# Key-query products on two 64-row halves of TensorE, with masked queries made once by ScalarE and VectorE, in an attention and expert kernel

## What is computed

```python
q = layernorm(x); k = v = ctx
ig, fg = gate projections of [q, k, v]           # per head and token
cs = cumsum(log_sigmoid(fg))
log_D = where(s >= t, cs[s] - cs[t], -inf) + ig[t]
m = max(log_D, axis=t)
qk = einsum('hsd,htd->hst', qh, kh) / sqrt(DH)   # DH = 16
C = qk * exp(log_D - m)
n = maximum(abs(sum(C, t)), exp(-m))
h = einsum('hst,htd->hsd', C / (n + EPS), vh)
x = x + layernorm(h) * ln_scale
x = x + experts(layernorm(x))                    # top 2 of 8, three layers, exact gelu
```

## Time and profile before

| | us |
|---|---|
| Median of 3 runs | 223.58 |
| Lowest and highest run | 218.94, 224.69 |
| Span of the profiled execution | 219.7 |

### The profile page before, as it was taken

The page is one execution under the profiler, slowest core; times in us unless marked ns, Lnnn a source line. Parts: engine busy times, 40 slices in busy tenths (PEclk is TensorE's granted clock), DMA queues, the critical chain, the costliest instruction groups (busy, mean ns, idle before and its releaser), DMA issues.

```text
span 219.7 us, 2995 instructions
## 1 busy us (share of the span) xinstructions
PE 180.9 (82%) x973; PEld 135.5 (62%) x973; DVE 156.7 (71%) x428; ACT 84.9 (39%) x160; POOL 128.5 (58%) x133
## 2 busy tenths in 40 slices
PE   7768899979999953676999999898998989999100
PEld 3464355554665722225999999696987969888000
DVE  2836243864866889927989999999999999955100
ACT  2352473430233011007366665727466374422100
POOL 6795033442501569474728787886978876445370
PEclk9969999975788555589999999999999999999855
DMA  5494019999920110010101120311203120021230
GB/s 163 118 364 143 12 28 339 375 371 360 358 69 1 49 38 10 0 49 16 30 0 31 15 28 22 30 30 13 32 19 30 30 25 8 5 30 12 24 26 5
DMA packets 19530, 18.16 MB, mean 83 GB/s; under 512 B 2232, under 2 KB 14008, under 8 KB 19512
## 3 DMA queue, kind: packets, MB, share of 16 engines
q1 hardware_dynamic: 15440, 15.22, 21.0%
q0 software_dynamic: 3712, 2.62, 9.1%
q10 hardware_dynamic: 360, 0.09, 0.2%
HBM read 15.07 MB, written 2.75 MB: 81 GB/s over the span
## 4 chain that ended last, share of the span: by engine, by line
DVE 42%; PE 29%; issue 15%; POOL 5%; DMA 4%; ACT 2%; SPq 0%; DVEq 0%; ACTq 0%; POOLq 0%
DVE wlo L917 12%; PE bank L1029 7%; PE bank L1060 7%; PE bank L1165 6%; DVE g1l L904 5%; DVE g2l L904 5%; DVE g1h L907 4%; POOL out_rows L438 3%; DVE g2h L907 3%; DVE qn L664 2%; DMA out_rows<-ys,ids 2%; PE bank L1004 2%; DMA xs<-in_x 2%; PE bank L1048 2%; PE bank L1049 2%
## 5 line engine op out<-in xcount | busy, mean ns | idle before, releaser
L438 POOL DMA_INDIRECT out_rows<-ys,ids x24 | 39.5, 1645 | 23.3 <-DVE ys L929 14.7
L578 ACT ACTIVATE g<-bank,smt 128x320 f32<-128x320 f32 x64 | 31.0, 527 | 52.4 <-PE bank L1165 35.0
L1165 PE MATMUL bank<-g1h,whi 128*128 128x320 f32 x128 | 41.7, 326 | 4.1 <-DVE g1l L904 3.9
L1165 PE MATMUL bank<-g1l,whi 128*128 128x320 f32 x128 | 39.5, 309 | 0.0
L1165 PE MATMUL bank<-g1h,wlo 128*128 128x320 f32 x128 | 39.5, 308 | 0.0
L917 DVE TENSOR_TENSOR wlo<-wraw,whi 128x512 fp32r<-128x512 f32 x32 | 32.7, 1064 | 0.8 <-ACT whi L535 0.8
L425 POOL DMA_INDIRECT xg<-xn_rows,ids x24 | 26.2, 1091 | 9.1 <-issue 5.5
L1165 PEld LDWEIGHTS bank<-g1h,whi 128*128 128x128 f32 x128 | 24.0, 188 | 8.5 <-issue 8.5
L383 POOL TENSOR_TENSOR wlo<-wraw,whi 128x512 fp32r<-128x512 f32 x16 | 24.2, 1525 | 7.7 <-ACT whi L535 7.6
L535 ACT ACTIVATE whi<-wraw 128x512 fp32r<-128x512 f32 x48 | 27.6, 623 | 0.3 <-issue 0.3
L904 DVE TENSOR_TENSOR g2l<-g,g2h 128x320 fp32r<-128x320 f32 x32 | 23.3, 729 | 1.1
(11 more groups left out here) (160 smaller groups left out, 306.1 us busy)
## 6 DMA issues: line engine op xcount, KB each, us to landing
wraw<-in_L_ffn_W SPq DMA_DIRECT2D x8, 1024.0 KB, 9.0
wraw<-in_L_ffn_W SPq DMA_DIRECT2D x16, 256.0 KB, 8.8
xs<-in_x SPq DMA_DIRECT2D x2, 256.0 KB, 3.6
cs_in<-in_ctx SPq DMA_DIRECT2D x2, 256.0 KB, 4.5
out_rows<-x SPq DMA_DIRECT2D x8, 64.0 KB, 2.1
xn_rows<-qn SPq DMA_DIRECT2D x8, 64.0 KB, 1.9
xg<-xn_rows,ids POOLq DMA_INDIRECT x24
out_rows<-ys,ids POOLq DMA_INDIRECT x24
```

What stands on the lines that cost most here:

```text
L438: g.indirect_dma_start(out=out, out_offset=bass.IndirectOffsetOnAxis(ap=ids[0:n, col:col + 1], axis=0), in_=ys[0:n, e % 2, c, :], in_offse ...
L578: a.activation(dst[:, m, :], bank[m][:, 0:MAIN], ACT.Gelu, bias=smt[:, col + MC * e + m:col + MC * e + m + 1]).then_inc(done, 1)
L1165: last = t.matmul(dst, wcol(w, p, layer, k, m), act_(k), start=(n == 0), stop=(n == 3 * ks - 1))
```

## The change

The masked queries of all batches are made once, ahead of the loop, as `qm`, with four head slots instead of eight: in slot h the rows of head h (in the upper 64 rows) and of head h + 4 (in the lower 64) stay, so each half of the rows carries four heads. The mask `hpick` has a column per slot. ScalarE makes batches 0 to 3 from PSUM bank 3, VectorE batches 4 to 7 from bank 4. `logits` runs two products of 64 rows, one on each half of the rows, each still 512 columns. `LT` and `RH` are 128 rows high, the rows from 27 on zero; GpSimd clears both whole, then writes ones in LT's first 27 rows. `select_heads` is moved on ScalarE. `hn` and `hl` use qT's space and `x2` that of `cs_in`. Several semaphores are merged into one with other counts (three scans into `scan_done`, four steps into `den_done`); these hunks are left out below.

```diff
-        LT = at("LT", [3 * NH + 3, B, S], BF16)
-        RH = at("RH", [3 * NH + 3, BH, S], BF16)
+        LT = at("LT", [128, B, S], BF16)
+        RH = at("RH", [128, BH, S], BF16)
         delta = at("delta", [3 * NH, NH])
-        qbd = at("qbd", [128, 2, NH, S])
+        qm = at("qm", [128, NH // 2, B, S])
...
-        hn = at("hn", [128, 2, 2, D])
-        hl = at("hl", [128, 2, 2, D])
+        hn = qT[:, 0:4, :].rearrange("p (a i) d -> p a i d", i=2)
+        hl = qT[:, 4:8, :].rearrange("p (a i) d -> p a i d", i=2)
...
-        x2 = at("x2", [128, B, D])
+        x2 = cs_in
...
                             pattern=[[DH, NH]], channel_multiplier=-1).then_inc(s.const_done, 1)
+            g.memset(LT[:].bitcast(F32), 0.0).then_inc(s.const_zero, 1)
             pool.wait_ge(s.const_done, 6)
-            g.memset(LT[:], 1.0).then_inc(s.lt_ones, 1)
-
-            def make_qbd(b):
-                if b >= 2:
-                    pool.wait_ge(s.qk_ps, 2 * (b - 1))
-                g.tensor_tensor(qbd[:, b % 2, :, :], qT[:, b:b + 1, :].to_broadcast([128, NH, S]),
-                                hmask[:].unsqueeze(2).to_broadcast([128, NH, S]), ALU.mult).then_inc(s.qbd_done, 1)
-            pool.wait_ge(s.qT_done, 1)
-            make_qbd(0)
+            g.tensor_tensor(hpick[:], hmask[:, 0:NH // 2], hmask[:, NH // 2:NH], ALU.add).then_inc(s.hpick_done, 1)
+            g.memset(RH[:].bitcast(F32), 0.0).then_inc(s.rh_zero, 1)
+            pool.wait_ge(s.const_zero, 9)
+            g.memset(LT[0:3 * NH + 3, :, :], 1.0).then_inc(s.lt_ones, 1)
...
-                if i == 0:
-                    make_qbd(1)
...
             for j in range(NP + 1):
-                if j + 1 < NP:
-                    make_qbd(2 * j + 2)
                 if j >= 1:
                     rsqrt(rs2, ve2, s.ve2_done, s.rs2_done, j - 1)
-                if j + 1 < NP:
-                    make_qbd(2 * j + 3)
...
+            act.wait_ge(s.hpick_done, 1)
+            for h in range(NH // 2):
+                a.activation(qm[:, h, 0:4, :], bank[3][:].rearrange("p (b t) -> p b t", t=S), ACT.Copy,
+                             scale=hpick[:, h:h + 1]).then_inc(s.qm_act, 1)
             act.wait_ge(s.delta_done, 1)
-            for b in range(3):
-                select_heads(b)
+            act.wait_ge(s.rh_zero, 1)
+            select_heads(0)
...
-            for b in range(3, 5):
+            for b in range(1, 4):
                 select_heads(b)
...
                 if j == 0:
+                    select_heads(4)
                     select_heads(5)
...
+            dve.wait_ge(s.hpick_done, 1)
+            dve.wait_ge(s.qT_done, 2)
+            for h in range(NH // 2):
+                v.tensor_scalar(qm[:, h, 4:8, :], bank[4][:].rearrange("p (b t) -> p b t", t=S), hpick[:, h:h + 1], None,
+                                ALU.mult).then_inc(s.qm_dve, 1)
+
             dve.wait_ge(s.gates_ps, 1)
...
             def logits(b):
 
-                pe.wait_ge(s.qbd_done, b + 1)
+                pe.wait_ge(s.qm_act, 4)
+                if b >= 4:
+                    pe.wait_ge(s.qm_dve, 4)
                 for half in range(2):
                     if 2 * b + half >= 3:
                         pe.wait_ge(s.cw_done, 2 * b + half - 2)
-                    t.matmul(qk_bank(b, half)[:], cT[:, b, :],
-                             qbd[:, b % 2, half * 4:half * 4 + 4, :].rearrange("p h t -> p (h t)"),
+                    rows = slice(64 * half, 64 * half + 64)
+                    t.matmul(qk_bank(b, half)[:].rearrange("p (h t) -> p h t", t=S), cT[rows, b, :], qm[rows, :, b, :],
                              start=True, stop=True).then_inc(s.qk_ps, 1)
...
                     pe.wait_ge(s.const_done, 6)
+                    pe.wait_ge(s.qm_dve, 4)
```

More of the change, by code:

```diff
@@ L82, in build @@
         hmask = sb("hmask", [128, NH])
+        hpick = sb("hpick", [128, NH // 2])
         minus_half = sb("minus_half", [128, NH])
@@ L206, in build @@
         qT_ps cT_ps qT_done cT_done wq_zero wpad_done v1_done gates_ps
-        fgt_done nabs_done expn_done softplus_done logf_done lsum_done u_done cm_done mld_done um_done em_done
+        fgt_done nabs_done expn_done softplus_done logf_done scan_done mld_done um_done em_done
         um1_done part_done emT_ps max_in lt0_in lt1_in lt_in emT_done emTe_done delta_done rh_done lt_ones
-        qbd_done qk_ps arg_ps dec_done cw_done pv_ps den1_done den2_done den_done rden_done hn_done st2_done mv2_done
+        hpick_done rh_zero qm_act qm_dve qk_ps arg_ps dec_done cw_done pv_ps den_done hn_done st2_done mv2_done
         ve2_done rs2_done hl_done x2_done st3_done mv3_done ve3_done rs3_done xn_done xnT_ps xnT_done score_ps
@@ L284, in _ @@
                              W3[e].rearrange("(k p) n -> p k n", p=128)).then_inc(w_in[e], 16)
-            sp.wait_ge(s.const_zero, 11)
+            sp.wait_ge(s.const_zero, 12)
             zeros = zrow[:].unsqueeze(1).to_broadcast([128, PAD // 128, D])
@@ L358, in _ @@
             g.memset(prefb[:, 0, :], 0.0).then_inc(s.const_zero, 1)
-            pool.wait_ge(s.const_zero, 11)
+            pool.wait_ge(s.const_zero, 12)
             g.affine_select(out=trib[:], in_=trib[:], compare_op=ALU.is_gt, fill=0.0, base=0,
@@ L682, in _ @@
             dve.wait_ge(s.const_zero, 6)
-            v.tensor_tensor_scan(lsum[:], ones64[:], logf[:], 0.0, ALU.mult, ALU.add).then_inc(s.lsum_done, 1)
-            dve.wait_ge(s.lsum_done, 1)
+            v.tensor_tensor_scan(lsum[:], ones64[:], logf[:], 0.0, ALU.mult, ALU.add).then_inc(s.scan_done, 1)
+            dve.wait_ge(s.scan_done, 1)
             v.scalar_tensor_tensor(out=um[0:BH, :], in0=pv_bank[0][0:BH, 0:S], scalar=gbias[0:BH, :], in1=lsum[:],
[L686 to L689, removed]
+                                   op0=ALU.add, op1=ALU.subtract).then_inc(s.scan_done, 1)
+            dve.wait_ge(s.scan_done, 2)
+            v.tensor_tensor_scan(cm[:], um[0:BH, :], um[0:BH, :], -3e38, ALU.max, ALU.max).then_inc(s.scan_done, 1)
+            dve.wait_ge(s.scan_done, 3)
             v.tensor_scalar(um[BH:128, :], cm[:], -1.0, None, ALU.mult).then_inc(s.um_done, 1)
@@ L725, in normalise_and_route @@
                     v.scalar_tensor_tensor(out=den1[:, p, :, :], in0=pv[:, :, :, DH], scalar=EPS_NORMALIZER, in1=floor,
-                                           op0=ALU.add, op1=ALU.max).then_inc(s.den1_done, 1)
+                                           op0=ALU.add, op1=ALU.max).then_inc(s.den_done, 1)
                     v.tensor_scalar(den2[:, p, :, :], pv[:, :, :, DH], -1.0, EPS_NORMALIZER, ALU.mult, ALU.add)\
-                        .then_inc(s.den2_done, 1)
+                        .then_inc(s.den_done, 1)
                 if route:
@@ L734, in normalise_and_route @@
                 if norm:
-                    dve.wait_ge(s.den1_done, j + 1)
-                    dve.wait_ge(s.den2_done, j + 1)
+                    dve.wait_ge(s.den_done, 4 * j + 2)
                     v.tensor_tensor(den[:, p, :, :], den1[:, p, :, :], den2[:, p, :, :], ALU.max).then_inc(s.den_done, 1)
@@ L741, in normalise_and_route @@
                 if norm:
-                    dve.wait_ge(s.den_done, j + 1)
-                    v.reciprocal(rden[:, p, :, :], den[:, p, :, :]).then_inc(s.rden_done, 1)
+                    dve.wait_ge(s.den_done, 4 * j + 3)
+                    v.reciprocal(rden[:, p, :, :], den[:, p, :, :]).then_inc(s.den_done, 1)
                 if route:
@@ L748, in normalise_and_route @@
                 if norm:
-                    dve.wait_ge(s.rden_done, j + 1)
+                    dve.wait_ge(s.den_done, 4 * j + 4)
                     v.tensor_tensor(hn[:, p, :, :].rearrange("p i (h c) -> p (i h) c", c=DH),
```

## The result

| | before | after |
|---|---|---|
| device time, median (lowest to highest), four runs each | 221.28 (218.94 to 224.69) | 209.28 (207.15 to 209.64) |
| ratio | 1 | 0.9455 [0.939, 0.9521] |
| profiled execution: span | 219.7 | 207.3 |
| first exponent product | 26.45 | 23.82 |
| first transpose of normalised rows (L1072, now L1076) | 46.81 | 40.21 |

The change saves 12.0 us by the medians and 12.4 us by the spans. The table splits the 12.4: 2.6 us ahead of the loop, 4.0 in the loop's first part (20.4 to 16.4 us), 5.5 in its second (27.4 to 22.0), 0.3 behind it. Single executions of one kernel differ here by 1 to 4%, in three experiments by 5 to 7%: of the four before, two took 219.0 us and two 223.6 and 224.7, and against the lower two alone the saving is 9.7 us.

The account below looks back on a forecast made before the run. No engine bounds the kernel end to end; the changed stage, the eight-batch loop, is TensorE's. Span 219.7 - 3.9 (loop's first part) - 3.3 (second) + 0 (ahead of it) = 212.5 us, 216.4 by the median; range 207 to 226.

Parts of the forecast that it names:

- starts stay in order: Loop's key-query products: second half's first instruction runs only beside first half's second; three slots, 1.48 us, saving 0.41 a batch.
- the 0 for the part ahead of the loop: Ahead of the loop, normalisation held by GpSimd memsets or freed from its two-input product: 0, bounds -3.1 and +2.4 us.
- The 3.9 us added to get from the span to the median: Whole kernel: profiled span 219.7 us lies 3.9 under the three-run median 223.58, so 3.9 is added at the end.
- rival B: TensorE's clock stays at 2.4 GHz to the end of attention: 209.7 us by the median; chance 0.18.
- Rival C: The key-query halves do not overlap; exponents and GpSimd leave about 3.5 us saved: 220.1 us by the median; chance 0.18.
- Exponents: Loop's exponent products padded to 128 rows: four cost 0.96 us, saving 0.25 a batch at full clock (bounds 0 and 0.4).
- The loop's first part: Up to the first transpose: 3.9 us saved, 2.6 of products, 1.3 of blocked VectorE and shorter stalls; about 16.5 us left.
- The second part: Loop from 46.8 to 74.1 us: 2.4 us from key-query and 0.9 from exponent groups, 3.3 saved; about 24 left.
- three key-query groups lose 0.8 each: Loop's second part: three key-query groups (3.76 to 3.49 us) lose 0.8 us each, 2.4 us together.
- D: Rival of the other sign: TensorE's clock falls sooner and doesn't return; 228.3 us by the median; chance 0.13.
- levels alternate as before: Forecast's clock assumption: in the loop's second part TensorE's clock levels alternate as before; forecast 216.4 us, chance 0.38.
- E: Rival ahead of the loop: RH's memset holds the last query normalisation, 2 us lost, rest as forecast; 218.4 us; chance 0.13.

Follow-up runs that it names:

- x_serial: Kernel after, with a wait so each batch's second 64-row key-query product starts only when the first has ended: median 231.8 us.
- x_pool_load: Kernel after, with six useless GpSimd products of the old masked-query (qbd) size where before made them: median 215.1 us.
- x_qbd_late: Kernel before, with GpSimd waiting for all eight query normalisations ahead of its first qbd product: median 218.2 us, ratio 0.9961.
- x_hold: Kernel after, with hpick made behind RH's clearing, so the LT and RH memsets stand back to back: median 211.9 us.
- x_rows27: Kernel after, with exponent products reading only the 27 data rows of the padded tiles: median 228.6 us, ratio to before 1.0417.
- x_fill_each: Kernel after, with one useless full-row product ahead of every exponent pair from batch 1 on (14 in all): median 209.0 us.
- x_pad_only: Kernel after, but queries masked by GpSimd and full-row key-query products as before; padding and clearings stay: median 218.3 us, ratio to before 0.9964.
- x_fill: Kernel after, with four useless full-row products in the wait at 40 us, ahead of the first transposes: median 211.1 us.
- x_rows27_fill: x_rows27 with one useless 128-row product ahead of each exponent pair from batch 1 on (14 in all): median 226.4 us.

## Why the prediction was right or wrong

The direction was right, and 209.3 us lies in the range. The forecast of 7.2 us saved was too small; 12.0 were. In spans, in which the sum was made, it had 212.5 us and 207.3 were measured. Of the 5.2 us missed, 2.6 lie ahead of the loop (forecast 0), 0.1 in its first part, 2.2 in its second, 0.3 behind it. So two steps failed: "starts stay in order", with the 0.8 us a group that follow from it, and the 0 for the part ahead of the loop. The 3.9 us added to get from the span to the median were a third, smaller error: after they are 2.0 (209.3 less 207.3), as the before median of 223.58 was of three executions, two of them high.

That 209.3 lies beside rival B's 209.7 is luck and no support for B: the clock did fall, at 43.1 us. Step by step:

**Key-query products: the step that failed is "starts stay in order".** It gave three slots, 1.48 us, by a choice between bounds, which leaned on a rule where no row bore on it. The lower bound, two slots and 1.03 us, was right: 1.07. Rival C, no overlap, falls with these rows and with x_serial. The Trainium skill ("TensorE: Matmul & The Clock Gate", Part 3, The mechanism) has products start and end strictly in program order. For the instructions the trace here disagrees: of first half, first half, second half, second half, the third starts beside the first (29.71 and 29.70), ahead of the second (30.24). The two products as wholes do start and end in order. The Trainium skill's page "TensorEngine Tiling (Array Packing)", Overview, with "up to 2x", is nearer to it.

**Exponents** were 0.25 us a batch in the forecast; 0.32 measured (1.19 to 0.87), the starts 0.22 apart as forecast.

**The loop's first part** took 16.4 us against 16.5 forecast, but two errors cancel. TensorE was done with its products 15.4 us after the loop's start, 0.5 sooner than forecast, and then waited 0.96 us, not 0.6, for VectorE. The path over VectorE sets this transpose, so the second slot saved brought little here. That this path got free of GpSimd is worth 2.4 us up to the first transpose and 4.2 us of the whole loop (x_pool_load); the forecast had 1.3, all of it ahead of the transpose.

**The second part** saved 5.5 us, not 3.3 (22.0 us, where about 24 was said). The term that was mis-sized is "three key-query groups lose 0.8 each": from start to start they took 3.69, 3.54 and 3.42 us before, 10.7 in all, and take 1.21, 2.01 and 1.07 now, 4.3. At half clock a group saves 1.7 us (3.69 to 2.01), not 0.8, which makes 5.0 of the 6.4; the rest is that two of the three groups fell on full clock, in this execution. The other work of this part, from which the forecast took 0.9 us for the exponents, got 0.9 us longer: two of its three exponent groups fell on half clock (1.7 us each).

**Ahead of the loop: the step that failed is the 0**, put between -3.1 and +2.4; it was -2.6. The question which instruction held the normalisation was the right one, but neither answer was. A memset alone holds it (1052 ns in x_qbd_late, 4123 in x_hold), and in the kernel before the hold went on through the two-input product behind the memset (3052 ns). What decided in these traces is whether GpSimd's long instructions stand back to back. Of the 2.3 us by which TensorE's gate products end sooner (15.37 instead of 17.64), VectorE's masks, put at nil as long as these products cover them, take 0.8 back. And I read only the longest L664 of the held instructions; the scan cm at 20.30, held by a qbd that was to vanish, was 1.1 us more, and it stood in the trace of before.

**The clock.** Rivals B and D were both of this kind, and the forecast (levels alternate as before) was right for this kernel. But the prediction priced the padding at 0.25 us a batch of exposed loads, and gave D, the clock that falls sooner, a chance of 0.13 without asking what kept it from happening. x_rows27 is D's case: 228.6 us, where D said 228.3. That the two agree to 0.3 us is luck: D had the fall at 38.2 us and the padding in place, and x_rows27 fell at 30.8 us without it. The padding is what keeps the change out of it. B, a clock that stays up to the end of attention, came about in x_fill_each, with fourteen more products: 9.4 to 10.1 us for two batches (transposes at 40.82, 50.95, 60.37), where B had 9.3, the last value product at 59.8 us, where B had 60, and 209.0 us, where B had 209.7. The kernel after is as fast with a clock that falls, so B was not needed for its time. E is x_hold: 2 us over the forecast was said, 2.6 over the kernel after was measured, within the noise, and 1.4 at the loop's start. The prediction's mark for D, "slower from a fall ahead of 38.4 us on", is not contradicted: x_rows27 fell at 30.8 us and x_serial, which has no overlap, at 37.3, both slower than before.

A sum over single profiled executions, of the loop alone, puts the parts side by side: before to x_pad_only (padding) -5.8 us; x_pad_only to x_pool_load (paired halves, GpSimd as loaded) +0.6; x_pool_load to after (GpSimd relieved) -4.2. In this order the pairing brings nothing by itself: its products are shorter, but the clock of the second stretch is 0.65 instead of 0.85, and VectorE's path sets the first. Whether it is needed for the relief of GpSimd, with its masks half as large, was not run. The order matters: taken out of the finished kernel, the padding is worth 17.7 us of loop (x_rows27), the pairing 20.0 (x_serial). They are not terms that add.

**What stays open.** Why the clock falls at 43 us in the kernel after, behind a stretch with TensorE busy 18.2 of 19.3 us, isn't settled. In x_fill, with the wait before it down to 0.32 us, it fell at 51.8 us, behind a wait of 1.80; but in x_hold, without any filling, it fell at 53.1, and neither was faster. How often the clock falls is partly a matter of the execution (x_rows27_fill, 215.6 to 229.7), and how far that bears on the sums of single executions above was not measured. That the number of rows bears on the clock is shown; by what, is not. Unpaired products on full rows without GpSimd's load were not run.

## What to carry to other kernels

Two float32 products on disjoint halves of the rows took half their time here (1.07 us, against 2.30, 0.2 of it hand-over, one after the other), though they were issued one behind the other; but where TensorE's clock is near its fall, first ask what halving the rows does to it. In this kernel it paid to keep the neighbours on all 128 rows, zeros included. Look for every VectorE instruction in the trace that is several times longer than its equals and see which GpSimd instruction lies beside it: taking that work away gave the excess back here, and so did, in one case, a short one between two long ones. Where two edits are tied by the clock, test them together and one by one: padding alone showed nothing here, all but the padding was 4% slower, and both together were 5.5% faster.

## What the runs showed of the hardware

- Two float32 products of 64 rows each, on rows 0 to 63 and 64 to 127, run as two pairs of instructions (starts 29.70, 29.71, 30.24, 30.24; 1.07 us instead of 2.30 with 0.2 of hand-over).
- TensorE busy without a pause can still be put at 1.2 GHz: in x_rows27 it fell at 30.8 us, in a stretch with 24.47 of 24.50 us busy, and stayed there for 31.60 busy us of 31.60. The number of rows in a product bears on it (mean clock 0.80 to 0.81, 0.84 to 0.86, 0.88 to 0.91 with 27, 64, 128 rows), rows of zeros count as rows, and with 28 useless full-row products the mean clock of x_rows27 rose to 0.85 to 0.91.
- A change of row count between neighbouring products (27 or 64 to 128 and back) exposes the weight load: starts 0.32 us apart, not 0.22, in both cases.
- A GpSimd memset holds a VectorE normalisation for its whole length, and two back to back hold it through both: 4123 ns beside 0.52 and 3.51 us. The Trainium skill ("SBUF — State Buffer", Who interferes with whom) says that of GpSimd and VectorE in its two-port modes whoever comes first has the shared ports for a whole instruction and the other blocks; the trace agrees (1052 ns beside a memset of 1.03 us, against some 340 undisturbed), and shows besides that the one that waits isn't let in between two long GpSimd instructions.
